# Reordering VectorE's work between two layers, and moving four scalings and casts of queries

## The reference

```
x = x + xattn0(layernorm(x), ctx)        # layer 0, one head
x = x + moe0(layernorm(x))               # 64 experts, 6 chosen, plus a shared expert
# layer 1, attention with 16 heads of 8 features, for each of 4 batches:
q = layernorm(x) @ Wq.T + bq ; k = ctx @ Wk.T + bk ; v = ctx @ Wv.T + bv
x = x + softmax(q k^T / sqrt(8)) v @ Wo.T + bo
x = x + moe1(layernorm(x))               # 8 experts, 2 chosen
```

## Time and profile before

| what | value |
|---|---|
| median of 3 runs | 314.22 us (313.34 to 314.53) |
| the profiled execution | 312.86 us, of which 311.0 us are the span |
| TensorE busy | 268.3 us, 86% |
| VectorE busy | 200.9 us, 65% |
| ScalarE busy | 140.2 us, 45% |
| mean granted clock of TensorE | 0.916 of full speed |

### The profile page before, as it was taken

How to read it: one execution, slowest core, us unless ns; L and a number is a source line. 1 busy time by engine, 2 the same in 40 slices (tenths; PEclk the granted TensorE clock), 3 DMA queues, 4 the chain that set the end, 5 groups by cost and what they waited for, 6 DMA issues and landing times.

```text
span 311.0 us, 5673 instructions
## 1 busy us (share of the span) xinstructions
PE 268.3 (86%) x2046; PEld 169.7 (55%) x2046; DVE 200.9 (65%) x633; ACT 140.2 (45%) x273; POOL 119.0 (38%) x152
## 2 busy tenths in 40 slices
PE   0998776699999999885489999999899999899983
PEld 0657533256888887662115455545344455777762
DVE  2567698938788544466797778765454848854335
ACT  1444332015555555523326777777554523243321
POOL 5867255788654440014211111120000057578720
PEclk9999697955999999996557999999999999999999
DMA  7943759145998789563606630006801001111143
GB/s 199 315 140 115 204 120 186 17 35 48 181 181 178 150 171 194 116 135 105 168 26 168 149 72 4 4 2 218 276 0 36 0 24 42 32 46 40 51 128 100
DMA packets 22911, 34.01 MB, mean 109 GB/s; under 512 B 3388, under 2 KB 14804, under 8 KB 22565
## 3 DMA queue, kind: packets, MB, share of 16 engines
q1 hardware_dynamic: 19523, 28.48, 34.0%
q0 software_dynamic: 2080, 4.07, 10.9%
q10 hardware_dynamic: 1282, 1.12, 1.4%
HBM read 23.56 MB, written 7.80 MB: 101 GB/s over the span
## 4 chain that ended last, share of the span: by engine, by line
PE 57%; DVE 17%; issue 11%; DMA 5%; ACT 5%; POOL 3%; ACTq 0%; DVEq 0%; POOLq 0%
PE bank L917 52%; DVE score L1901 3%; POOL xg L612 2%; DMA packc<-in_packc 2%; DMA big<-q_parts 1%; DMA xg<-normalised,slot_token 1%; PE bank L1247 1%; DVE xn L1498 1%; ACT pbuf L902 1%; DVE x L1985 1%; POOL rstd L562 1%; DMA q_parts<-parts 1%; ACT pbuf L734 1%; DVE st L1485 1%; PE bank L1203 1%
## 5 line engine op out<-in xcount | busy, mean ns | idle before, releaser
L1901 DVE TENSOR_REDUCE score<-bank 128x2 f32<-128x512 f32 x64 | 41.9, 686 | 13.2 <-PE bank L917 12.4
L612 POOL DMA_INDIRECT xg<-normalised,slot_token x32 | 38.1, 1190 | 24.3 <-PE bank L1063 11.3
L863 ACT ACTIVATE pbuf<-bank 128x512 f32<-128x512 f32 x64 | 37.1, 598 | 15.5 <-PE bank L917 15.1
L917 PE MATMUL bank<-ks,big 128*128 128x256 bf16 x128 | 29.1, 319 | 5.4 <-DVE score L1901 3.7
L562 POOL TENSOR_TENSOR rstd<-veps,mhalf 128x4 f32<-128x4 f32 (+1 forms) x10 | 9.0, 900 | 61.7 <-DVE veps L1490 59.6
L917 PE MATMUL bank<-big,ks 128*128 128x256 bf16 x128 | 24.8, 281 | 0.4 <-ACT pbuf L863 0.4
L917 PEld LDWEIGHTS bank<-ks,big 128*128 128x128 bf16 x128 | 9.6, 104 | 24.4 <-DVE score L1901 13.9
L627 POOL CAST nmp<-score 128x16 bf16<-128x16 f32 x8 | 1.6, 198 | 49.1 <-DVE score L1901 49.1
L1620 DVE TENSOR_TENSOR pbuf<-rk,iota_s 128x4096 bf16<-128x4096 bf16 (+1 forms) x10 | 18.5, 1855 | 2.7 <-DMA xg<-normalised,slot_token 2.6
L917 PE MATMUL bank<-pbuf,vaug 128*9 128x256 f32 x256 | 19.7, 381 | 0.0
L656 POOL DMA_INDIRECT xg<-normalised,sslot x12 | 11.5, 957 | 21.4 <-DVE sslot L1834 18.0
(11 more groups left out here) (240 smaller groups left out, 579.0 us busy)
## 6 DMA issues: line engine op xcount, KB each, us to landing
big<-in_w SPq DMA_DIRECT2D x8, 704.0 KB, 7.5
big<-in_w SPq DMA_DIRECT2D x8, 384.0 KB, 8.9
big<-in_ew SPq DMA_DIRECT2D x12, 256.0 KB, 5.6
ks<-k_parts SPq DMA_DIRECT2D x2, 1024.0 KB, 10.1
big<-ks SPq DMA_DIRECT2D x8, 256.0 KB, 5.0
big<-q_parts SPq DMA_DIRECT2D x8, 256.0 KB, 4.1
k_parts<-parts SPq DMA_DIRECT2D x2, 768.0 KB, 4.6
q_parts<-parts SPq DMA_DIRECT2D x8, 192.0 KB, 2.4
```

What stands on the lines that cost most here:

```text
L612: pool.indirect_dma_start(out=xg[:, g % 2, j, :], out_offset=None, in_=xn_dram, in_offset=bass.IndirectOffsetOnAxis(ap=slot_token[:, g % N ...
L863: a.activation(prob1[:, e % NPROB, :], bank[2 + e % 2][:, :], ACT.Exp).then_inc(a_exp, 1)
L917: return pe.matmul(out_, lhsT, rhs, start=start, stop=stop, skip_group_check=True)
L1901: v.tensor_reduce(nm1[:, c, 2 * hp:2 * hp + 2], bank[m % 2][:, :].rearrange("p (h k) -> p h k", h=2), X, ALU.max, negate=True).then_inc(a_ ...
```

## The change

VectorE's list between the layers is reordered; the first normalisation goes ahead of the second statistics, the second normalisation behind the third residual, and the query of batch 0 ahead of the third statistics. ScalarE does the bias and scale of batches 2 and 3 (with a bias that VectorE scales once at the start of the stretch) and casts their first part right behind; the second cast moves to steps 19 and 23, the two subtractions on VectorE to steps 18 and 22, and 20 and 24. SyncE writes and loads the queries of batches 2 and 3 behind k = 1 and 2 in place of 0 and 1. One exponential of a single column on ScalarE ahead of the loop makes the table load come there. TensorE's and GpSimd's lists stay as they are.

```
+QUERY_REST = {19: 2, 23: 3}
...
             for k in range(2 * NB):
                 maxima_stacked(k)
-                if k < 2:
-                    queries_stacked(2 + k)
+                if 1 <= k < 3:
+                    queries_stacked(1 + k)
                 if 2 <= k < 2 + PLANES:
                     plane_zeros(k - 2)
...
-            def query_parts(b):
-
+            def scaled_queries(b):
+                a.wait_ge(q1_f, b)
+                a.wait_ge(q1_ps, b + 1)
+                a.activation(qf[:, batch(b)], bank[6 + b % 2][:, 0:TB], ACT.Identity,
+                             bias=bias_q1[:, 0:1], scale=SCALE1).then_inc(q1_f, 1)
+
+            def query_first(b):
                 a.wait_ge(q1_f, b + 1)
                 a.copy(parts[:, 0, batch(b)], qf[:, batch(b)]).then_inc(q1_hi, 1)
+
+            def query_second(b):
                 a.wait_ge(q1_res, b + 1)
                 a.copy(parts[:, 1, batch(b)], query_rest(b)).then_inc(q1_mid, 1)
...
             norm_transposed(7)
-            query_parts(2)
-            query_parts(3)
+            for b in (2, 3):
+                scaled_queries(b)
+                query_first(b)
...
+            a.activation(rsg[:, 0:1], zero[:, :], ACT.Exp)
             for s in range(SLOTS):
                 m, e = s, s - LAG
+                if s in QUERY_REST:
+                    query_second(QUERY_REST[s])
...
+            def query_bias():
+                v.wait_ge(ld_small, 64)
+                v.tensor_scalar(bias_q1[:, :], biases[:, B_BQ1:B_BQ1 + 1], SCALE1, None, ALU.mult)
...
+            query_bias()
             residual2(0)
             statistics2(0)
             residual2(1)
+            normalise(4)
             statistics2(1)
-            normalise(4)
+            residual2(2)
             normalise(5)
-            residual2(2)
+            queries(0)
+            query_residual(0)
             statistics2(2)
-            queries(0)
+            query_last(0)
             residual2(3)
-            query_residual(0)
+            queries(1)
             normalise(6)
-            query_last(0)
+            query_residual(1)
             statistics2(3)
-            queries(1)
-            query_residual(1)
+            query_last(1)
             normalise(7)
-            query_last(1)
...
-                for i, step in enumerate((queries, query_residual, query_last)):
-                    if s in (i, i + 1):
-                        step(2 + s - i)
+                if s + 1 in QUERY_REST:
+                    query_residual(QUERY_REST[s + 1])
+                if s - 1 in QUERY_REST:
+                    query_last(QUERY_REST[s - 1])
```

More of the change, by code:

```diff
@@ L133, in build @@
         mhalf = sb("mhalf", [P, 4])
+        bias_q1 = sb("bias_q1", [P, 1])
         zero = sb("zero", [P, 1])
@@ L825, in _ @@
             norm_transposed(5)
-            query_parts(0)
+            query_first(0)
+            query_second(0)
             a.wait_ge(z_T, 3)
             norm_transposed(6)
-            query_parts(1)
+            query_first(1)
+            query_second(1)
             a.wait_ge(z_T, 4)
             norm_transposed(7)
-            query_parts(2)
-            query_parts(3)
+            for b in (2, 3):
+                scaled_queries(b)
+                query_first(b)
             a.wait_ge(ln_tsb, 8)
```

## The result

The changed kernel takes 315.59 us in the median of 20 runs (314.09 to 318.77), the kernel before 313.85 us in 20 runs beside them (310.93 to 314.97). The ratio is 1.0092, 95% interval 1.0067 to 1.0118: slower by 0.7 to 1.2% (the ratio compares the runs and is not the quotient of the two medians). The profiled execution took 315.99 us, its span 313.8 us, 2.8 more than the span before.

What follows compares the result with a forecast made beforehand. It took batch 0's query chain and TensorE's queue to bound the seam, and VectorE's maxima the first 17 steps. Terms 0.6 + 0 + 0.3 + 0.2 = +1.1 us on 314.22 gave 315.3, range 313.0 to 317.2.

Steps and rivals of the forecast that it cites:

- (a): Rival: later loop start and work taken out of its first steps nearly cancel; about 0.35% slower, inside 0.5%; chance 0.50.
- (b): Rival: at step 41 TensorE waits for rows behind batch 3's loads and zeros; up to +2.1 us; chance 0.28.
- The seam: Between the layers: max_scores(0) starts at 151.8 instead of 149.18, 2.6 us later, with TensorE's queue deciding.
- Steps 0 to 17: Loop start: query work gone from the first steps saves 2.0 us, leaving step 4 0.6 later; term +0.6 us.
- The table: ScalarE ahead of the loop: moving the 1.28 us table load out of an idle stretch gains nothing; term 0.
- Steps 18 to 24: Loop: two VectorE subtractions a batch, partly in idle time, cost 0 to 0.68 us; term +0.3 us.
- Step 41: Loop: rows of maxima_stacked(3) issued later behind loads and zeros stall TensorE between 0 and 0.8 us; term +0.2 us.
- the third sign of being wrong: The prediction is wrong if the loop loses more than 1 us between steps 18 and 45.
- (c): Rival: the clock falls before 140.58, batch 0's multiplications take 1.22 instead of 0.60; +1.7 us, 315.9; chance 0.07.
- (d): Rival: the fourth normalisation doesn't decide, the loop starts with the load at 150.26; -0.4 us, 313.8; chance 0.08.
- (e): Rival: the loop starts at its old 149.2 and the 2.0 us saved stay; about -1.7 us, 312.5; chance 0.07.

Runs made afterwards that it cites:

- e1: The kernel before with only VectorE's new list order between the layers; ratio to before 1.0085, median 316.40 us.
- e4: The changed kernel with the fourth statistics ahead of query_residual(1) and the fourth normalisation ahead of query_last(1); ratio to before 1.0051, median 315.45 us.
- e6: The changed kernel with queries1(0) ahead of batch 1's transposes in TensorE's list; ratio to before 1.0084, median 315.86 us.
- e2: The changed kernel with VectorE's old list order between the layers, all other moves kept; ratio to before 0.9992, median 313.62 us.
- e5: The changed kernel with VectorE's old order between the layers and the zeros behind k = 4 and 5; ratio to before 0.9967, median 312.22 us.
- e8: The kernel before with only the early one-column exponential that loads the table; ratio to before 1.0014, median 314.66 us.
- e11: The changed kernel with batch 3's writes ahead of the rows of k = 2 and its loads behind them; ratio to before 1.0049, median 314.58 us.
- e10: The changed kernel with batch 3's query loads moved behind k = 3, writes and zeros staying; ratio to before 0.9985, median 314.12 us.
- e3: The changed kernel with the zeros behind k = 4 and 5 in place of 2 and 3; ratio to before 1.0046, median 314.27 us.
- e7: The changed kernel with TensorE's, ScalarE's and VectorE's orders putting batch 0 first, batch 3's loads and zeros late; ratio to before 0.9938, median 311.52 us.
- e9: e7 with queries1(3) behind max_scores(1) in TensorE's list in place of ahead of max_scores(0); ratio to before 0.9871, median 310.77 us.

## Why the prediction was right or wrong

**The time** was 315.59 for a forecast of 315.3 and lies inside the range. That it is so near is in part luck. The forecast put +1.1 us on a median of 314.22. The change cost more than that, +1.7 by the medians and +2.2 behind the first residual of the profiles, and the kernel before took 313.85 in the runs beside it, 0.4 less. **The case** was not the likeliest one: (a) said about 0.35% slower, inside 0.5%; it became 0.92%, case (b), slower by the wait at step 41.

**The seam, right in its steps.** From the first residual, the second normalisation was forecast at 4.64 and came at 4.56; batch 0's query 6.21, came 6.13; the new idle time of VectorE 1.5, came 1.54; the fourth normalisation 13.75, came 13.72; the loop 16.8, came 16.60, behind `queries1(3)`. e1 shows that this alone makes the kernel 0.85% slower; e4 and e6 show the two places, the idle time ahead of `query_residual(1)` and TensorE's order.

**Steps 0 to 17, right.** Forecast +0.6 at step 4 and on; it came to +0.5: step 4's maximum is at 152.90 + 4 x 0.697 = 155.69, 20.06 behind the first residual, and was 19.58 behind it. Step 17 came at 164.26, 1.11 later than before and just outside the 1 us that the prediction named, but 0.62 of that lies ahead of the first residual. e2 and e5 show the 2.0 saved without the seam's loss.

**The table, right.** e8: no change.

**Steps 18 to 24, a little low.** +0.3 forecast, +0.5 measured; from the start of step 17's scores to step 24's it took 6.00 before and 6.53 after. At least a part goes with the clock, back 5 us behind step 17's start and not 3: e6 and e11, with the same moves, took 6.00 as before. What the two subtractions cost by themselves isn't shown.

**Step 41, the step that failed.** The term was +0.2 with 0.8 as its upper end, and it came to 1.35. With it the third sign of being wrong came true: between steps 18 and 45 the loop lost 1.90 us (24.09 before, 25.99 after), where the prediction named 1 as the most. I had taken the landing of batch 3's writes and the issue of three rows from the earlier trace rows; both grew. The third write took 3.39 from the start of its issue to its landing, and SyncE issued nothing else meanwhile; the rows took 3.37 to issue, not 2.38. Without the sitting (e10) there is no wait. Without the zeros (e3) 0.29 us are left. Sitting and zeros act together, and either edit takes most of the loss away. The Trainium skill, DMA: Bandwidth & Descriptors, section "Queues, rings and completion order", says that a semaphore increment lands only behind earlier writes of the same DMA engine. The trace shows little of it here: the last row took 2.11 us from issue to its reader with the loads and zeros ahead of it, and 2.77 in e3 with the loads alone. The larger share of the delay was ahead of that, in SyncE's waiting and issuing, which that rule doesn't name.

No edit settles why the third write lands later in the moved place, but the traces show which part of it is late. In the ten kernels that have it there it took 3.4 to 4.2 us, in before, e1 and e8 2.2 to 2.3, and batch 2's took 2.0 in the changed kernel. The 512 KB of batch 2's loads alone don't explain it: they were issued 3.43 ahead of the first write in the changed kernel (172.83, 176.26) and 3.57 ahead in before (164.91, 168.48). SyncE waits for 48 semaphore increments from a batch, 16 for each write. In e2, 46 of batch 3's 48 were there at 175.89, 1.97 behind the issue of the third write; the last two came at 177.77 and 178.09. What the DMA engines moved in e2 from 172.9 to 178.1 (GB/s in slices of 0.13 us), and in e11 from 173.4 to 178.2 (slices of 0.12 us):

```profile
GB/s 158 114 138 12 63 32 0 87 331 339 354 339 327 327 323 331 308 331 319 296 4 0 0 0 0 0 4 8 12 8 12 16 20 20 24 20 16 0 0 0
```

```profile
GB/s 0 239 205 307 34 273 205 410 307 376 205 239 205 307 205 205 252 235 265 77 192 214 256 277 316 341 346 333 350 346 333 303 278 231 158 179 13 0 34 0
```

In e2 about 330 GB/s flow until 175.5, almost nothing until 176.3, and then never more than 24, which is about a sixteenth of 330: this fits one of the 16 DMA engines being behind while the others are done. A transfer of instructions of 16 KB runs there from 175.46 to 176.38, and the rest of the write moves where it ends. The other eight kernels of this kind (changed, e3 to e7, e9, e10) show the same: such a transfer beside the writes, two or three of the 48 increments late, the first of them 1.1 to 1.4 us behind the end of the transfer (changed kernel: 177.62 to 178.83, increments at 179.97, 180.26 and 180.86). In the changed kernel, e4 and e5 the third write was also slow to issue (1.56, 1.99 and 2.30 us, 0.54 to 0.56 in the other six). Before, this transfer ran at 177.10, when batch 3's writes had landed at 171.80, beside zeros that nobody waited for. e11 is slow in another way: no increment is late by itself, the 48 come one behind the other from 176.58 to 178.15, all three writes take 3.5 to 3.7 us, and mostly 200 to 400 GB/s are moved until 177.5; its writes stand 1.19 behind 512 KB of loads. So e11 doesn't speak against the transfer of instructions as the cause in the other nine. That it is the cause is inferred from these nine traces; no run moved it alone.

**Rivals.** (c), the clock falling before 140.58, did not occur: the granted clock of the changed kernel was 1.00 in the windows from 140 to 142, and it fell inside 142 to 143 as before. (d) and (e) are excluded by step 0 at 16.60.

## What to carry to other kernels

Moving one engine's work to the front gains nothing while another engine's list keeps the old order: read the queue of every engine that the moved step passes through, and reorder them together. VectorE's new order alone made the kernel 0.85% slower (e1). With the other engines' lists reordered too (e7) the loop started as early as with the old lists (e5), and it started 1.0 us earlier when the step that set the start, `queries1(3)`, was moved out of the way (e9). What else makes e7 and e9 faster than before (0.6% and 1.3%) are the queries of batches 2 and 3 taken out of steps 0 to 3, with zeros and loads late enough. In a queue that waits for its own writes, the price of a moved transfer is the whole sitting time (3.39 us here), and what stands behind it pays. Place transfers that nobody needs soon behind the small ones that somebody does.

## What the runs showed of the hardware that was not expected

A row transfer of 4 KB took 1.59 us to issue on SyncE right behind 512 KB of loads and 512 KB of zeros, and 0.67 for the one ahead of it; in e2, e4 and e6, with the same ahead, that second row took 1.87, 1.62 and 1.79, and 0.67 in e3 and e5, which have no zeros there. Beside a transfer of instructions of 16 KB, two or three of the 48 increments of a batch's writes came late and the whole batch waited for them (nine kernels). A wait of 1.87 us on TensorE in the middle of the loop was followed by the granted clock at 0.5 for more than 3 us and 1.5 us more of time (e2), while waits of 1.19, 1.43 and 2.25 us (changed kernel, e4, e6) were not followed by it. The first residual, at the end of the same layer 0, came between 133.87 and 137.29 in the profiled executions; in the changed kernel's the granted clock was at 0.5 inside 132 to 135 there, in the one of before at 1.0.
